# Transposing DMAs in place of TensorE transposes for the normalised rows of a fused two-stage kernel

## The reference

```python
def fake_quant(x, s, z):
    return (clip(round(x / s + z), 0, 255) - z) * s

def stage1(x, ctx):          # 2 x 2048 x 2048 ctx
    return matmul(fake_quant(layernorm(x)), fake_quant(ctx))

def stage2(h, A, B, Wr):     # 4 experts of rank 16
    logits = h @ Wr.T                     # 4 per row
    gates = softmax(top 2 of logits)
    mid = einsum('tf,erf->ter', h, A)     # 64 per row
    return 4 * sum_e gates_e * (mid_e @ B_e.T)

x = x + tanh(g_xattn) * stage1(x, ctx)
x = x + tanh(g_ffn) * stage2(layernorm(x), A, B, Wr)
```

## Time and profile before

| | |
|---|---|
| median of 3 runs | 429.81 us |
| profiled execution | 432.26 us, span 430.5 us |
| PE busy | 360.3 us (84%) |
| DVE busy | 334.7 us (78%) |
| ACT busy | 257.6 us (60%) |
| POOL busy | 85.5 us (20%) |
| mean DMA rate | 159 GB/s |
| first 77 us (context of batch element 0, tiles 0 and 1) | PE follows the loads |
| slots 2 to 7 (context of batch element 1 still loading) | 22.5 to 22.9 us each |
| slots 9 to 14 | 21.0 us each |

### The profile page before, as it was taken

The page is one execution under the profiler, slowest core; times in us unless marked ns, Lnnn a source line. Parts: engine busy times, 40 slices in busy tenths (PEclk is TensorE's granted clock), DMA queues, the critical chain, the costliest instruction groups (busy, mean ns, idle before and its releaser), DMA issues. The chain is left out here.

```text
span 430.5 us, 7428 instructions
## 1 busy us (share of the span) xinstructions
PE 360.3 (84%) x2480; PEld 213.2 (50%) x2480; DVE 334.7 (78%) x764; ACT 257.6 (60%) x240; POOL 85.5 (20%) x74
## 2 busy tenths in 40 slices
PE   0063549679989998989899999999999999999954
PEld 0031224265555555555556464756565656565642
DVE  2549994897897979797979787879787878687584
ACT  1655698377859587776767455556464655555140
POOL 1000000130404030222222222222222222224020
PEclk9996779868999999999999999999999999999995
DMA  4999980246755645556472222222222222312022
GB/s 142 344 402 428 424 311 4 97 142 246 251 162 180 190 159 202 185 189 201 150 240 99 99 99 98 99 98 97 97 97 97 97 97 97 99 50 97 2 97 99
DMA packets 22241, 68.52 MB, mean 159 GB/s; under 512 B 3204, under 2 KB 3716, under 8 KB 20100
## 3 DMA queue, kind: packets, MB, share of 16 engines
q1 hardware_dynamic: 22216, 68.20, 44.4%
HBM read 51.42 MB, written 16.78 MB: 158 GB/s over the span
## 5 line engine op out<-in xcount | busy, mean ns | idle before, releaser
L539 PE MATMUL ps_main<-q,q1T 128*128 128x512 f16 x928 | 213.3, 381 | 0.0
L539 PEld LDWEIGHTS ps_main<-q,q1T 128*128 128x128 f16 x928 | 88.1, 99 | 101.9 <-issue 8.5
L404 ACT ACTIVATE h_hi<-x,small_tile 128x1024 f16<-128x1024 f32 x32 | 39.4, 1234 | 65.5 <-DVE small_tile L830 65.5
L349 POOL TENSOR_TENSOR h_lo<-work,h_hi 128x1024 f16<-128x1024 f32 x31 | 66.6, 2148 | 43.7 <-ACT work L409 41.9
L814 DVE SCALAR_TENSOR_TENSOR x<-ps_main,small_tile,xt 128x512 f32<-128x512 f32 x60 | 44.8, 747 | 23.8 <-DMA out_x<-x 14.5
L788 DVE BATCH_NORM_STATS2 small_tile<-xt 128x6 f32<-128x512 f32 x64 | 40.8, 683 | 16.8 <-DMA xt<-in_x 16.7
L343 POOL TENSOR_TENSOR small_tile<-small_tile 128x1 f32<-128x1 f32 x16 | 8.8, 549 | 210.3 <-DVE small_tile L826 210.3
L392 ACT ACTIVATE work<-xt,small_tile 128x1024 uint8<-128x1024 f32 x32 | 38.1, 1234 | 16.0 <-DVE small_tile L804 16.0
L819 DVE BATCH_NORM_STATS2 small_tile<-x 128x6 f32<-128x512 f32 x64 | 44.3, 692 | 1.7
L888 DVE TENSOR_TENSOR x<-ps_delta,x 128x512 f32<-128x512 f32 x64 | 42.3, 683 | 2.7 <-PE ps_delta L605 2.7
L382 ACT ACTIVATE ctx_stage<-ctx_stage,small_tile 128x1024 uint8<-128x1024 f32 x32 | 38.7, 1236 | 5.0 <-DMA ctx_stage<-in_ctx 5.0
(11 more groups left out here) (98 smaller groups left out, 401.9 us busy)
## 6 DMA issues: line engine op xcount, KB each, us to landing
xt<-in_x SPq DMA_DIRECT2D x32, 512.0 KB, 3.7
q<-in_ctx SPq DMA_DIRECT2D x16, 1024.0 KB, 17.8
ctx_stage<-in_ctx SPq DMA_DIRECT2D x32, 512.0 KB, 5.0
out_x<-x SPq DMA_DIRECT2D x64, 256.0 KB, 2.2
x<-in_L_ffn_A SPq DMA_DIRECT2D x1, 512.0 KB
x<-in_L_ffn_B SPq DMA_DIRECT2D x1, 512.0 KB, 15.9
small_tile<-in_L_xattn_x_scale SPq DMA_DIRECT2D x2, 0.5 KB, 4.2
small_tile<-in_L_xattn_x_zp SPq DMA_DIRECT2D x2, 0.5 KB, 4.7
```

Of the source, the lines that this page charges most:

```text
L349: nc.gpsimd.tensor_tensor(h_lo[:, h, :], work[:, h, :], h_hi[:, h, :], ALU.subtract).then_inc(h_lo_ready, 1)
L404: nc.scalar.activation(h_hi[:, h, :], x1[:, b % 2, half(h)], ACT.Identity, bias=h_bias[:, :], scale=h_rstd[:, :]).then_inc(h_hi_ready, 1)
L539: mm = pe.matmul(acc[:, :], q1T[:, b % 2, k, :], q2[:, batch(b), k, cols(n)], start=(k == 0), stop=(k == KT - 1))
```

## The change

For the tiles 0 to 14 the 32 PE transposes of `h_hi` and `h_lo` and the three copies that follow them go. In their place SP issues four transposing DMAs per tile, each from `h_hi[:, h]` or `h_lo[:, h]` (128 x 1024 f16, 256 KB) straight into `hT[:, h]`. The mids wait for the DMAs' semaphores. `mid_hi` of both halves now stands where `turn_hi` stood, ahead of `main(b, 2)`; behind `main(b, 2)` come both `turn_q1`, then both `mid_lo`, then `main(b, 3)`. The last tile keeps its PE transposes (`turn_last`, the wait of which is now on `q1T_ready` and `hiT_ready`). In SP's queue the four DMAs take places of their own, and `store_out(b - 2)` and `load_x(b + 2, 0)` stand behind the two for the high part. `high_part` and `low_part` wait for the DMA that read their buffer.

```diff
@@ block.sync
+            def turn_hi(b, i, h):
+                wait(sp, h_hi_ready, b, i, 2, h + 1)
+                sp.sem_inc(sp_waited, 1)
+                wait(sp, lo_used, b, i, 2, h - 1)
+                sp.sem_inc(sp_waited, 1)
+                sp.dma_start_transpose(hT[:, h, :, :], h_hi[:, h, :]).then_inc(hiT_loaded[h], 16)
+            def turn_lo(b, i, h):
+                wait(sp, h_lo_ready, b, i, 2, h + 1)
+                sp.sem_inc(sp_waited, 1)
+                wait(sp, hi_used, b, i, 2, h + 1)
+                sp.sem_inc(sp_waited, 1)
+                sp.dma_start_transpose(hT[:, h, :, :], h_lo[:, h, :]).then_inc(loT_loaded[h], 16)
...
+                if b == 1:
+                    load_x(b + 2, i, 0)
+                    turn_hi(b - 1, i, 0)
+                    turn_hi(b - 1, i, 1)
+                    turn_lo(b - 1, i, 0)
+                    turn_lo(b - 1, i, 1)
+                    ctx_half(0)
+                    load_x(b + 2, i, 1)
+                    store_out(b - 1, i, (0, 1))
...
                 if 3 <= b < TILES - 1:
                     load_x(b + 1, i, 1)
-                if b >= 2:
-                    store_out(b - 2, i, (2, 3))
+                turn_hi(b - 1, i, 0)
+                ctx_half(0)
+                turn_hi(b - 1, i, 1)
+                store_out(b - 2, i, (2, 3))
                 if b < TILES - 2:
                     load_x(b + 2, i, 0)
...
+                turn_lo(b - 1, i, 0)
+                turn_lo(b - 1, i, 1)
                 ctx_half(1)
                 ctx_half(2)
                 ctx_half(3)
-                if b >= 2:
-                    store_out(b - 1, i, (0, 1))
+                store_out(b - 1, i, (0, 1))
@@ block.gpsimd, low_part
-                wait(pool, lo_turned, b, i, 2, h - 1)
+                wait(pool, loT_loaded[h], b, i, 16, 0)
@@ block.scalar, high_part and slot
-                wait(act, hi_turned, b, i, 2, h - 1)
+                wait(act, hiT_loaded[h], b, i, 16, 0)
+                wait(act, h_lo_ready, b, i, 2, h - 1)
...
                 scale(1)
                 scale(2)
-                copy_hiT(b - 1, i, 0)
-                copy_hiT(b - 1, i, 1)
                 if ahead:
                     scale_x(b + 1, i, 0)
                     scale_x(b + 1, i, 1)
-                copy_loT(b - 1, i)
@@ block.tensor, slot
                         main(b, i, 1, general)
-                        turn_hi(b - 1, i, 0)
-                        turn_hi(b - 1, i, 1)
+                        mid_hi(b - 1, i, 0)
+                        mid_hi(b - 1, i, 1)
                     main(b, i, 2, general)
                     if b == 1:
-                        turn_hi(b - 1, i, 0)
-                        turn_hi(b - 1, i, 1)
-                    for h in range(2):
-                        mid_hi(b - 1, i, h)
-                        turn_lo(b - 1, i, h)
-                    for h in range(2):
-                        mid_lo(b - 1, i, h)
-                        if b < TILES - 1:
-                            turn_q1(b + 1, i, h)
+                        mid_hi(b - 1, i, 0)
+                        mid_hi(b - 1, i, 1)
+                    if b < TILES - 1:
+                        turn_q1(b + 1, i, 0)
+                        turn_q1(b + 1, i, 1)
+                    mid_lo(b - 1, i, 0)
+                    mid_lo(b - 1, i, 1)
                     main(b, i, 3, general)
```

More of the change, by code:

```diff
@@ L543, in main, with turn_last @@
                 mm.then_inc(main_done, 1)
-            def turn_h(b, i, h, src, ready, turned, free, per, extra):
-                if ready is not None:
-                    wait(pe, ready, b, i, 2, h + 1)
-                wait(pe, free, b, i, per, extra)
+            def turn_last(h, src, turned):
                 for k in range(HK):
@@ L551, in turn_h, with turn_hi_last, turn_lo_last, mid_hi @@
                 mm.then_inc(turned, 1)
-            def turn_hi(b, i, h):
-                if b == TILES - 1:
-                    turn_h(b, i, h, h_hi, h_hi_ready, hi_turned, loT_ready[h], 1, 0)
-                    return
-                turn_h(b, i, h, h_hi, h_hi_ready, hi_turned, q1T_ready, 2, 3 + h)
-            def turn_lo(b, i, h):
-                if (b, h) == (TILES - 1, 1):
-                    pe.wait_ge(last_low_ready, 1)
-                    turn_h(b, i, h, h_lo, None, lo_turned, hiT_ready, 2, 1 + h)
-                    return
-                turn_h(b, i, h, h_lo, h_lo_ready, lo_turned, hiT_ready, 2, 1 + h)
-            def mid_hi(b, i, h):
-                wait(pe, hiT_ready, b, i, 2, h + 1)
+            def turn_hi_last(b, h):
+                pe.wait_ge(h_hi_ready, 2 * b + h + 1)
+                pe.wait_ge(q1T_ready, 2 * TILES)
+                turn_last(h, h_hi, hi_turned)
+            def turn_lo_last(b, h):
+                if h == 0:
+                    pe.wait_ge(h_lo_ready, 2 * b + 1)
+                else:
+                    pe.wait_ge(last_low_ready, 1)
+                pe.wait_ge(hiT_ready, h + 1)
+                turn_last(h, h_lo, lo_turned)
+            def mid_hi(b, i, h):
+                if b == TILES - 1:
+                    pe.wait_ge(hiT_ready, h + 1)
+                else:
+                    wait(pe, hiT_loaded[h], b, i, 16, 16)
                 if h == 0:
@@ L580, in mid_lo @@
             def mid_lo(b, i, h):
-                wait(pe, loT_ready[h], b, i, 1, 1)
+                if b == TILES - 1:
+                    pe.wait_ge(loT_ready[h], 1)
+                else:
+                    wait(pe, loT_loaded[h], b, i, 16, 16)
                 for k in range(HK):
```

63 lines of the change are left out of this document (32 added, 31 removed).

## The result

The changed kernel takes 495.2 us (median of 4 runs, 493.1 to 499.7) against 430.9 us for the kernel before, measured beside it: a ratio of 1.150 (95% interval 1.146 to 1.155), 64 us slower. The forecast was 459.2 us with a range of 427 to 520. Sign and range held; the forecast loss of 29.4 us was less than half of what came, and the time lies above the 445 to 485 us that the forecast gave itself within that range. The medians in this text are of all executions; the ratios leave out an execution that lies more than 1.5% above the fastest of its kernel.

A forecast was written before the change was run, and what follows sets the result against it. PE's own list was taken to bound slots 9 to 15, and with a 1.38 us wait nearly all of slots 2 to 7; ideal slot 19.15 us. Terms 5.6 + 22.5 + 1.3 = 29.4 on 429.81 gave 459.2 us, range 427 to 520.

The forecast's parts named there:

- 1.4 us for that rounding: Every slot: DVE's rounding ends 1.4 us after `main(b, 2)`, so the second `turn_q1` waits, 0.9 us in slot 9.
- L: Time from a transposing DMA's issue to its landing, taken as 3.7 us like the 512 KB load of `x`.
- q: Time for which a DMA holds SP, taken as 1.0 us, midway between 0.35 and 1.5.
- Rival A: Transposing DMAs as cheap as a store (landing 2.2 us, SP held 0.35): 424 to 432.5 us, likeliest 426; chance 0.14.
- rival D: Transposing DMAs one after another become the bound, from about 4 us each: about 590 us; chance 0.12.
- C: Rival: slow DMAs (landing 6 us, SP held 2) and PE's clock lost everywhere: 505 us; chance 0.22.
- slot 1, taken at 0: Slot 1: four DMAs replace PE transposes and ACT copies where PE idled 7 us; between -2 and +3, taken at 0.
- slots 2 to 6, forecast +22.5: Slots with context loads: late second high half and half clock make 27.2 us against 22.7, +4.5 in each of five.
- costliest line: Slots 2 to 6: the second `turn_hi` stands behind `ctx_half(0)`, which waits for DVE; PE waits 5.2 us.
- slots 7 to 14, forecast +6.1: Slot 7 +1.3, slot 8 about nothing, later slots 21.8 us against 21.0, +0.8 each, mostly from late low halves.
- SP is through with `load_x` at offset -3.6: Slots 8 to 15: SP issues the high halves at -3.6 and -2.0; the second lands at 1.7, PE waits 1.0 us.
- Pushed back by at most 2q ahead of waits that end later anyway: nothing: Old stores and loads, delayed in SP's queue, were taken to cost nothing while q stays under about 2.

The follow-up runs named there:

- p4_slot1: Changed kernel with tile 0's four transposing DMAs taken ahead in SP's queue, among slot 0's context loads: 486.9 us, ratio 1.130.
- q1_ctx_small: Changed kernel with the context rows loaded inside slots 0 to 6 cut to a quarter of their bytes: 477.5 us, ratio 1.108.
- the filler: Changed kernel with twelve thrown-away matmuls ahead of `mid_hi` in slots 2 to 7: 492.9 us, ratio 1.138.
- p7_x_first: Changed kernel with the second half of `x` loaded at the end of the slot before, ahead of the stores: 484.7 us, ratio 1.127.
- the combined version: Changed kernel with tile 0's DMAs ahead, `ctx_half(0)` behind both `turn_hi`, rounding ahead of `add_main(b, 2)`, `x` early from slot 7: 456.4 us, ratio 1.059.

## Why the forecast was right and where it failed

**Right: what bounds the kernel, and the sign.** PE's list was the slot, and everything late lengthened it: in slot 9 the 19.85 us of busy PE and its four waits (1.69, 1.06, 1.33 and 0.27 us) make the 24.2. The list that is left is 19.85 us and not 19.15; spread over the four waits, the 0.7 us are some 0.2 us for each restart, an estimate, which the differences of starts in a full list could not show. Waits stand where the forecast put them: `mid_hi` behind the DMA with half clock after it, `turn_q1` behind DVE's rounding (1.06 us, forecast 0.9), the low mids last. The 1.4 us for that rounding were read from the start of `add_main`, which itself starts 0.3 us or more behind the end of `main(b, 2)`; measured are 1.7 from there.

**Nearly right: L and q.** 3.7 and 1.0 were forecast, 4.2 and about 1.25 are the medians. For q that was luck: its upper bound of 1.5 was half of the 3.09 us that the earlier trace rows gives for a pair, and those are the time from the first start to the last end; each of the two held SP for 0.33 us. L and q are not where the size was lost: with plain copies, at a landing of 4.0, the kernel is only 10 to 15 us faster. Rival A (landing like a store) fell since even a plain copy of 256 KB lands in 4.0 us at this place; rival D fell since a transposing DMA holds SP for 1.25 us and lands in 4.2, where it needed about 4 for each in a chain; C's mechanism, the clock lost in the slots without context, showed in slots 7 and 8 (clock 0.87) and in part in 12 and 13 (0.93), and slots 9 to 11 ran at 1.00. That 495 lies near C's 505 and inside the range is not C come true: its L of 6 and q of 2 are not the medians, and slot 1, which it took at 0 too, holds 11.6 us of the loss.

**Failed: slot 1, taken at 0 and measured at +11.6.** The prediction's step looked at PE's idle time there and not at SP's queue. The four DMAs had been put behind slot 0's four `ctx_half`, each of which waits for DVE. `p4_slot1` gives 10.8 of it back. What the prediction left out was the queue: for each step that moves to a new queue, what it is put behind there.

**Mis-sized: slots 2 to 6, forecast +22.5, measured +28.8.** `ctx_half(0)` between the two `turn_hi` was called the costliest line. It is worth 2 us a slot and not the 5.2 of wait that were put to it, since the first high half was late as well, by 2.3 to 5.0 us. The forecast let it be in time, with an L that counted no bytes ahead of the first half. With a quarter of the context's bytes these slots are 11 us shorter (`q1_ctx_small`). The clock was under-sized: the forecast lost 1.7 us a slot to it, and PE's busy time in these slots is 22.0 to 22.7 us where slot 9 has 19.85 at full clock, 2.7 more in the mean. Of that the filler gave back 1.6 and 2.1 us in the two slots in which it kept the clock.

**Failed: slots 7 to 14, forecast +6.1 in all, measured +26.0.** Here the term was "SP is through with `load_x` at offset -3.6". That was right for when the transfers are handed over (slot 9: the first at -3.75, the second at -1.9, forecast -3.6 and -2.0). But the 512 KB of that load are in the same rings, so the first half lands 5.6 us later and the second 4.5, and not 3.7. The mids start at 1.86, `main(b, 2)` ends at 6.8 and not 5.9. And the load of `x` was taken as untouched: it became late itself (5.1 us, 3.5 before), DVE waited 3.06 us for it (1.40 before), the next load came at offset 5.3 and not 3.7, and with it the low halves, the second of which let PE go at 11.3 and not 8.7. That is 2.6 us at the place that sets the slot, and slot 9 (24.2) missed its forecast (21.8) by 2.4. Moving the one load took all of it away in slots 8 to 14 (`p7_x_first`). Slot 7 stayed at 27.9 us there and at 26.0 in the combined version, in which the load still stands ahead of it; what its +4.8 consists of is not shown. "Pushed back by at most 2q ahead of waits that end later anyway: nothing" was the wrong sentence: it counted when the old transfers are handed over, and what they lost is how fast they land with the new ones behind them.

**Open.** Of the 26 us that remain in the combined version, the runs show where they lie (slots 2 to 7, rings at 86% in slot 2) and, in the changed kernel, that fewer bytes help. How they divide between bytes, the clock (0.93 to 0.94 in these slots) and the chain high, mid, low, mid wasn't measured there. Open is also why the first loads take longer in some of the kernels: slot 1 starts between 74.6 and 83.1 us, with the same DMAs in the same order before it. Nor was it tried to have two `hT` buffers, by which the low DMAs would not wait for the high mids.

## What to carry to other kernels

Before work is moved from a full engine to a DMA, write down for that DMA's place what stands ahead of it twice: the waits ahead of it in the issuing engine's list, and the bytes ahead of it in the rings, and add to the old transfers what the new one puts ahead of them. A landing time read from a page holds for the queue in which it was read; the same plain copy of 256 KB took 2.2 to 8.3 us here depending on what was ahead of it. Then do the move in part: half of it, with the consumer placed a long matmul later, and only where the rings were busy for less than half of the time, was the version that won, by 6 to 8 us of 430.
